# Paged attention of a conditioned residual block: value pages, queries and outputs in 2 KB rows, first key pages requested early

## The reference

```
B, S, HID = 32, 32, 512           # sequences, new tokens of each, features
D, HQ, HK = 128, 32, 8            # head size, query heads, key/value heads
PAGES, PSIZE, NPP = 64, 32, 16    # cache pages, tokens of a page, pages of a sequence
x = x + L0(x); x = x + L1(x); x = x + L2(x)
q, k, v = x @ Wq.T, x @ Wk.T, x @ Wv.T        # 32, 8 and 8 heads of 128
q, k = rope(rmsnorm(q)), rope(rmsnorm(k))
kc = k_cache[block_table]; vc = v_cache[block_table]       # 512 cached tokens of each sequence
scores = q @ concat(kc, k) * SCALE            # 544 keys; cached ones beyond cache_seqlens masked
o = softmax(scores) @ concat(vc, v)
out = x + o @ Wo.T
```

## Time and profile before

| | us |
|---|---|
| median of 3 executions | 1288.35 |
| lowest, highest | 1285.35, 1296.21 |
| the profiled execution | 1295.23 |
| its span (first to last instruction) | 1293.5 |

### The profile page before, as it was taken

The page is one execution under the profiler, slowest core; times in us unless marked ns, Lnnn a source line. Parts: engine busy times, 40 slices in busy tenths (PEclk is TensorE's granted clock), DMA queues, the critical chain, the costliest instruction groups (busy, mean ns, idle before and its releaser), DMA issues. The chain is left out here.

```text
span 1293.5 us, 28328 instructions
## 1 busy us (share of the span) xinstructions
PE 1194.0 (92%) x8010; PEld 1041.7 (81%) x8010; DVE 848.0 (66%) x1756; ACT 678.0 (52%) x1572; POOL 734.5 (57%) x572
## 2 busy tenths in 40 slices
PE   4987999999999699999999999999999994599997
PEld 2733888888888598899989998989899993487786
DVE  3677777777776576777777877777777764322222
ACT  2056444444443476777777777776777764211111
POOL 2030899999999655555555655555655541244442
PEclk9988999999999999999999999999999997799999
DMA  9302344344446699999999999999999946677772
GB/s 298 131 25 91 98 123 133 99 124 131 133 135 196 193 278 272 286 275 288 291 277 284 291 276 283 290 275 286 279 284 294 279 125 224 223 203 216 214 219 86
DMA packets 280080, 275.13 MB, mean 213 GB/s; under 512 B 57285, under 2 KB 242629, under 8 KB 280038
## 3 DMA queue, kind: packets, MB, share of 16 engines
q1 hardware_dynamic: 270278, 250.15, 66.8%
q10 hardware_dynamic: 9504, 24.44, 6.6%
q0 software_dynamic: 256, 0.03, 0.0%
HBM read 228.26 MB, written 46.27 MB: 212 GB/s over the span
## 5 line engine op out<-in xcount | busy, mean ns | idle before, releaser
L1208 ACT ACTIVATE att_prob<-att_neg,att_nmax 128x544 f32<-128x544 f32 x256 | 191.5, 748 | 157.7 <-DVE att_nmax L1028 156.0
L869 POOL TENSOR_TENSOR att_k_lo<-att_kT,att_k_hi 128x544 fp32r<-128x544 f32 x128 | 177.7, 1388 | 143.4 <-ACT att_k_hi L1231 142.7
L869 POOL TENSOR_TENSOR att_k_lo<-all_room_a,att_k_hi 128x544 fp32r<-128x544 f32 x124 | 171.1, 1381 | 128.1 <-ACT att_k_hi L1231 127.5
L1028 DVE CUSTOM_DVE_ANT_1 att_neg<-att_mask,pa_pair 128x576 f32<-128x576 f32 x256 | 192.2, 751 | 73.8 <-PE pa_pair L109 66.1
L1080 DVE COPY att_pT<-pa_pt 128x512 f32<-128x512 f32 x256 | 175.7, 687 | 23.6 <-PE pa_pt L899 23.6
L107 PE MATMUL pa_pair<-prj_wt_hi,early_xT_lo 128*128 128x512 f32 (+1 forms) x512 | 179.9, 351 | 6.4 <-DVE prj_wt_lo L1090 6.4
L108 PE MATMUL pa_pair<-prj_wt_lo,early_xT_hi 128*128 128x512 f32 (+1 forms) x512 | 174.5, 341 | 0.0
L109 PE MATMUL pa_pair<-prj_wt_hi,early_xT_hi 128*128 128x512 f32 (+1 forms) x512 | 172.9, 338 | 0.0
L107 PE MATMUL pa_pair<-att_k_hi,att_q_lo 128*128 128x288 f32 (+1 forms) x512 | 169.1, 330 | 1.1 <-POOL att_k_lo L869 1.1
L1439 POOL TENSOR_TENSOR out_o_n<-out_o_n,all_room_b 128x1024 f32<-128x1024 f32 x32 | 79.1, 2471 | 140.2 <-DMA all_room_b<-inv_scratch 140.2
L899 PE MATMUL pa_pt<-all_ident,att_prob 128*128 128x128 f32 x1024 | 154.0, 273 | 1.5 <-ACT att_prob L1208 1.5
(11 more groups left out here) (143 smaller groups left out, 2623.9 us busy)
## 6 DMA issues: line engine op xcount, KB each, us to landing
all_room_a<-in_k_cache_t SPq DMA_DIRECT2D x256, 128.0 KB, 4.1
att_kT<-in_k_cache_t SPq DMA_DIRECT2D x256, 128.0 KB, 3.5
all_room_b<-in_L_cond_v_cache SPq DMA_DIRECT2D x166, 128.0 KB, 3.5
att_vc<-in_L_cond_v_cache SPq DMA_DIRECT2D x160, 128.0 KB, 3.5
q_scratch<-prj_qst SPq DMA_DIRECT2D x64, 256.0 KB
o_scratch<-att_ost SPq DMA_DIRECT2D x32, 512.0 KB, 5.3
out_o_n<-o_scratch SPq DMA_DIRECT2D x32, 512.0 KB, 3.6
all_room_b<-inv_scratch SPq DMA_DIRECT2D x32, 512.0 KB, 5.7
```

Source lines behind the costliest of these rows:

```text
L869: g.tensor_tensor(k_lo[j % SPLITS][:], kT[j // HK % 2][:, :, j % HK, :], f32(k_hi[j % SPLITS][:]), ALU.subtract).then_inc(k_split, 1)
L1028: v.tensor_tensor_reduce(halves[0], halves[1], ps[j % 2][:, :, 0:KA], 1.0, 3.0e38, ALU.add, ALU.min, nmax[j % 2][:]).then_inc(maxed, 1)
L1208: act.activation(prob[j // GROUP % 2][:, j % GROUP, :], neg[j % 2][:, 0:KEYS], ACT.Exp, bias=nmax[j % 2][:, 0:1], scale=-1.0, accum_out=to ...
```

## The change

Four things are changed.

- **Value pages** lie in SBUF as [half, chunk, four heads x 128] in place of [chunk, eight heads x 128]. A page comes by one DMA as before, but each 4 KB row of it is now two pieces of 2 KB. TensorE's operand is addressed accordingly.
- **Queries** lie in scratch as [batch, d, head, 128] in place of [batch, head, d, 128]; the load of a batch's queries becomes two DMAs, each of four heads (2 KB per partition contiguous on both sides). The stores of the projection still write 512 B runs, now 4 KB apart.
- **Outputs** of a batch are stored by two DMAs of four heads each (2 KB rows), the first between the key pages and the value pages, with waits and semaphores per half.
- **Key pages of batches 0 and 1** (32 DMAs) are no longer requested two by two beside the last two heads' tiles, but all at once before the projection loop.

```
+GROUP = 4
+KQ_LOADS = PG + HK // GROUP
 def load_new_keys(eng, q_d, k_d, b, q, tile, sem):
-    eng.dma_start(q[:], q_d[bass.ds(b, 1)].rearrange("a h d x -> d (a h) x")).then_inc(sem, 16)
+    for g in range(HK // GROUP):
+        h = slice(g * GROUP, (g + 1) * GROUP)
+        eng.dma_start(q[:, h, :], q_d[bass.ds(b, 1), :, h, :].rearrange("a d h x -> (a d) h x")).then_inc(sem, 16)
 def load_value_page(eng, inp, tile, j, page, sem):
-    eng.dma_start(tile[r, j // PPT, :], v_pages[bass.ds(page, 1)].rearrange("a s c -> (a s) c")).then_inc(sem, 16)
+    src = v_pages[bass.ds(page, 1)].rearrange("a s (g x) -> (a s) g x", g=HK // GROUP)
+    eng.dma_start(tile[r, :, j // PPT, :], src).then_inc(sem, 16)
...
-        vc = [vc0, after_w1.sb("vc1", [P, NCH, HK * D])]
+        vc = [vc0, after_w1.sb("vc1", [P, HK // GROUP, NCH, GROUP * D])]
...
-                    sp.dma_start(q_d[tile, bass.ds(c, 1)].rearrange("b a d x -> d (b a) x"),
+                    sp.dma_start(q_d[tile, :, bass.ds(c, 1), :].rearrange("b d a x -> d (b a) x"),
...
                         for i in range(2 * t, 2 * t + 2):
-                            load_key_page(sp, inp, kT[0], i, pages0[i], kq_in[0])
...
-                    elif tail:
-                        for i in range(2 * t, 2 * t + 2):
-                            load_key_page(sp, inp, kT[1], i, pages1[i], kq_in[1])
...
                 pages0 = pages_of(nc, table, 0, 0, NPP, mybir.EngineType.SP)
                 pages1 = pages_of(nc, table, 1, 0, NPP, mybir.EngineType.SP)
+                for i in range(NPP):
+                    load_key_page(sp, inp, kT[0], i, pages0[i], kq_in[0])
+                for i in range(NPP):
+                    load_key_page(sp, inp, kT[1], i, pages1[i], kq_in[1])
                 loop(sp, body)
...
+                def store_out(b, slot, g):
+                    sp.wait_ge(o_staged, b * (HK // GROUP) + g + 3)
+                    cols = slice(g * GROUP * P, (g + 1) * GROUP * P)
+                    sp.dma_start(o_d[bass.ds(b, 1), :, cols].rearrange("a d x -> (a d) x"),
+                                 ost[slot][:, g * GROUP:(g + 1) * GROUP, :].rearrange("p h x -> p (h x)")
+                                 ).then_inc(o_stored[slot * (HK // GROUP) + g], 16)
...
                             load_keys(sp, b + 2, slot, pages)
+                        store_out(b, slot, 0)
+                        if not tail:
                             sp.wait_ge(valued, (b + 1) * HK)
                             load_values(sp, b + 2, slot, pages)
-                        sp.wait_ge(o_staged, (b + 1) * (HK // GROUP) + 2)
-                        sp.dma_start(o_d[bass.ds(b, 1)].rearrange("a d x -> (a d) x"),
-                                     ost[slot][:].rearrange("p h x -> p (h x)")).then_inc(o_stored[slot], 16)
+                        store_out(b, slot, 1)
...
-    q_d = nc.dram_tensor("q_scratch", [B, HK, D, QS], F32).ap()
+    q_d = nc.dram_tensor("q_scratch", [B, D, HK, QS], F32).ap()
```

More of the change, by code:

```diff
@@ L572, in stage_project_attend @@
                          wo, wo_in, q_d, k_d, v_d, o_d, inv_d):
-    GROUP = 4
     UNROLL = 2 * HK
@@ L696, in stage_project_attend @@
         o_staged = m.sem("o_staged")
-        o_stored = [m.sem(f"o_stored{i}") for i in range(2)]
+        o_stored = [m.sem(f"o_stored{i}") for i in range(UNROLL // GROUP)]
         cq, sn_q, ck, sn_k = (tabs[:, i] for i in range(4))
@@ L802, in _ @@
                 pages1 = pages_of(nc, table, 1, 0, NPP, mybir.EngineType.SP)
-                for slot in range(2):
-                    sp.sem_inc(o_stored[slot], 16)
+                for i in range(NPP):
+                    load_key_page(sp, inp, kT[0], i, pages0[i], kq_in[0])
+                for i in range(NPP):
+                    load_key_page(sp, inp, kT[1], i, pages1[i], kq_in[1])
+                for i in range(UNROLL // GROUP):
+                    sp.sem_inc(o_stored[i], 16)
                 loop(sp, body)
@@ L831, in _ @@
                 sp.wait_ge(inv_stored, 32)
+                for i in range(UNROLL // GROUP):
+                    sp.wait_ge(o_stored[i], (B // 2 + 1) * 16)
                 for slot in range(2):
-                    sp.wait_ge(o_stored[slot], (B // 2 + 1) * 16)
                     sp.wait_ge(wo_in[slot], 16)
@@ L913, in values @@
                     s, h = j // HK % 2, j % HK
-                    cols = slice(h * D, (h + 1) * D)
+                    cols = slice(h % GROUP * D, (h % GROUP + 1) * D)
                     o = po[j // GROUP % 2][:, j % GROUP * P:(j % GROUP + 1) * P]
@@ L917, in values @@
                     for c in range(NCH):
-                        pe.matmul(o, vc[s][:, c, cols], pT[j % 2][:, c, :], start=(c == 0 and j % GROUP == 0), stop=False)
+                        pe.matmul(o, vc[s][:, h // GROUP, c, cols], pT[j % 2][:, c, :], start=(c == 0 and j % GROUP == 0), stop=False)
                 def new_values(j, group):
@@ L1044, in split_q_hi @@
                     if g * GROUP % HK == 0:
-                        dve.wait_ge(kq_in[g * GROUP // HK % 2], (it + g * GROUP // UNROLL + 1) * 16 * (PG + 1))
+                        dve.wait_ge(kq_in[g * GROUP // HK % 2], (it + g * GROUP // UNROLL + 1) * 16 * KQ_LOADS)
                     src, hi, lo = q_part(g, it)
@@ L1229, in split_k @@
                     if j % HK == 0:
-                        act.wait_ge(kq_in[j // HK % 2], (it + j // UNROLL + 1) * 16 * (PG + 1))
+                        act.wait_ge(kq_in[j // HK % 2], (it + j // UNROLL + 1) * 16 * KQ_LOADS)
                     act.activation(k_hi[j % SPLITS][:], kT[j // HK % 2][:, :, j % HK, :], ACT.Copy).then_inc(k_hi_done, 1)
@@ L1293, in unit @@
                         act.wait_ge(valued, (group + 1) * GROUP)
-                        if g % 2 == 0:
-                            act.wait_ge(o_stored[j // HK], (it + 1) * 16)
+                        act.wait_ge(o_stored[g], (it + 1) * 16)
                         act.activation(ost[j // HK][:, g % 2 * GROUP:(g % 2 + 1) * GROUP, :],
@@ L1503, in program @@
         kT0 = room_a[:].rearrange("p (j h t) -> p j h t", j=PG, h=HK)
-        vc0 = room_b[:].rearrange("p (c x) -> p c x", c=NCH)
+        vc0 = room_b[:].rearrange("p (g c x) -> p g c x", g=HK // GROUP, c=NCH)
         q0 = m.sb("q0", [P, HK, QS])
```

## The result

| | before | after |
|---|---|---|
| median (us) | 1292.28 | 1328.92 |
| lowest, highest (us) | 1285.35, 1300.12 | 1326.8, 1336.41 |
| ratio to before, 95% interval | | 1.031, 1.0269 to 1.0351 |
| the profiled execution, its span (us) | 1295.23, 1293.5 | 1326.8, 1325.1 |

The changed kernel is 3.1% slower, 36.6 us. The prediction had the direction and 22.5 us of it; the result lies 2 us above the upper end of its range.

A forecast was written before the change was run, and what follows sets the result against it. SyncE's instruction stream was taken as the bound; passes of 20.32 us gave +23.0 us, with -3.0 at the beginning of attention and +2.5 in the projection: +22.5 us, 1310.9 us on the median; 8-in-10 range 1276 to 1327.

The forecast's parts named there:

- What bounds the kernel now: Attention passes: the length of SyncE's instruction stream is the bound, 19.28 us of its own work per pass.
- The second query load: One more DMA in every attention pass, ahead of the key pages: +0.58 us per pass, bounds 0.5 and 0.6.
- the second output store: One more store in every attention pass, register work and wait included: +0.66 us per pass.
- Value pages in two pieces: Ten value page issues per attention pass with one more dimension: +0.015 us each, 0.15 per pass, bounds 0 and 0.3.
- What may come back: Key page issues and table load in SyncE's pass get quicker: 0.35 us per pass taken, of at most 1.9.
- The beginning of attention: With early key pages, SyncE's 4.2 us wait for batch 0's values goes, less 1.24 us of added issues: -3.0 us.
- The beginning of the projection: First tiles: early key pages delay the stores and TensorE stands 3.2 us, bounds 0 and 6; taken as +2.5 us.
- (A): Attention: DMA engines are the bound, not SyncE's issuing; about 1288 us, range 1279 to 1298; chance 0.24.
- (B): Attention: 2 KB rows relieve the DMA engines so much that SyncE's pass shortens; 1267 us, range 1259 to 1279; chance 0.16.
- (C): Attention and projection: nothing comes back and every added cost is at its upper bound; 1329 us; chance 0.10.
- What the profile after would show: Trace signs: passes 20.3 us, no first-pass wait for `valued`, VectorE's waits 78 us, TensorE stall near 155 us, DMA share at most 0.95.

## Why the prediction was right in direction and short by 14 us

**What bounds the kernel now: right where the stream grows.** Three tiny DMAs cost 1.17 us of pass for 1.32 us of SyncE. What the step missed is how near the other limits stand: take work away, and waits for `valued` fill the place. For a change that only adds work this side doesn't matter.

**The second query load, the second output store: right, a little high.** 0.86 - 0.40 = 0.46 us in place of 0.58, and 722.30 - 721.84 = 0.46 in place of 0.66. The estimate of 0.66 had register work in it that isn't repeated.

**Value pages in two pieces: the step that failed.** It took 0.015 us for each page, with an upper bound of 0.03, from the queries' row (0.40 us, three dimensions). Measured: 0.564 - 0.370 = 0.19 us for each, and 5.81 - 4.03 = 1.8 us per pass, twelve times the 0.15 and six times the bound. The queries' DMA fills 128 partitions, and its pieces are apart in HBM alone: in SBUF they lie side by side, the form that the value pages split in HBM later showed to be cheap. So it was no bound for 32 partitions with two pieces 8 KB apart in SBUF, and no row of before shows that form. Two other rows of the kernel before could have warned that the form matters, the projection's stores of queries and of new values:

```profile
L773 SPq DMA_DIRECT2D q_scratch<-prj_qst x64: 387/398/467, 142.6 to 447.8; - x64
...
L778 SPq DMA_DIRECT2D v_scratch<-prj_vst x64: 561/592/1662, 143.8 to 448.8; - x64
```

A store of a single 512 B run per partition costs 592 ns there, more than any load of attention, so an upper bound of 0.03 us on a new form had no row behind it. ScalarE's price (0.258 us more for each of six) wasn't named at all; SyncE's own sums close the pass without it.

**What may come back: too low.** 0.35 us was taken of at most 1.9, with the longer pass named as the reason. Per pass the table load gave back 0.75, the key pages 0.56, the new keys 0.44 - 0.33 = 0.1, in all 1.4 us. The new keys are no relief of the DMA engines: the issue of that unchanged DMA takes 436 to 440 ns at its quickest in all kernels whose queries come in 512 B pieces ahead of it, and 332 ns in all with the new query layout (from 500 us on). Both places named in that step are the right ones, but the slower pace explains only 0.18 us of the key pages (tiny DMAs). The table load is shorter with the split store (alone: 2.24 to 1.39), and the key pages' issues with 2 KB value rows (alone: 6.15 to 5.69).

The two errors are of opposite sign. With the measured terms, 19.28 + 0.46 + 0.46 + 1.78 - 1.4 = 20.58, and 2.9 / 29 = 0.1 of waits: 20.7 us, against 20.79 measured (20.64 from the third pass on) and 20.32 predicted. Without the value pages' error the forecast would have been wrong the other way: the sum had 20.32 - 0.15 = 20.17 us for a cheap form, and the run with one shows 19.19. So the right direction was luck in part: with value pages as cheap as the sum had them, the kernel gets faster, and what made it slower is the term that the sum put at next to nothing.

**The beginning of attention: the mechanism seen, the gain not.** VectorE and SyncE where attention begins, to be read against the earlier trace rows:

```profile
443.39 0.42 DVE L1060 CAST att_q_hi<-att_q 128x512 fp32r<-128x512 f32 x1
...
451.17 0.58 SPq L777 DMA_DIRECT2D q_scratch<-prj_qst  x1
...
458.48 0.89 SPq L541 DMA_DIRECT2D all_q<-q_scratch  x2
...
460.08 9.37 SPq L548 DMA_DIRECT2D all_room_a<-in_k_cache_t  x16
...
470.20 0.56 SPq L742 DMA_DIRECT2D att_vd<-v_scratch  x1
470.86 7.02 SPq L557 DMA_DIRECT2D all_room_b<-in_L_cond_v_cache  x10
```

The stall of 11.50 us ahead of the cast has gone, and so has SyncE's wait for the values of batch 0. But the keys of batch 2 leave at 460.08 in place of 457.25 (the value pages that SyncE issues ahead of them have the dear form too), and the stall comes back one batch later. VectorE's cast for batch 2, then TensorE behind it:

```profile
475.92 0.43 DVE L1060 CAST att_q_hi<-all_q 128x512 fp32r<-128x512 f32 x1 [9.96 <-DMA all_room_a<-in_k_cache_t]
```

```profile
477.98 2.08 PE L931 MATMUL pa_pair<-att_pT,att_vc 128*128 128x128 f32 x8 [6.69 <-DVE att_pT L1093]
```

Before, that cast ran at 471.46 after 0.15 us of waiting. TensorE is then late with the values of batch 1, SyncE waits 2.5 us for them in the second pass, and that pass lasts 24.65 us in place of 19.99. The prediction had named this ("what is late next is that") and priced nothing for it. Up to the third pass's table load its terms give 2.5 - 3.0 + 0.79 = +0.3 us; measured are 503.3 - 497.4 = +5.9. From there on, 28 x (1.17 - 0.79) = 10.6 us are missing. Together the forecast is 16.2 us short by the traces and 14.1 by the medians, a difference within the spread of the last stage.

**The beginning of the projection: right.** SyncE, then TensorE, at the first tiles, beside the earlier trace rows:

```profile
128.73 8.08 SPq L548 DMA_DIRECT2D all_room_a<-in_k_cache_t  x16
136.99 8.05 SPq L548 DMA_DIRECT2D att_kT<-in_k_cache_t  x16
...
146.75 0.41 SPq L777 DMA_DIRECT2D q_scratch<-prj_qst  x1
...
154.89 0.40 SPq L777 DMA_DIRECT2D q_scratch<-prj_qst  x1
...
155.61 1.17 PE L982 MATMUL pa_pair<-all_ident,prj_qn 128*128 128x128 f32 x5 [2.19 <-ACT prj_qst L1281]
```

The stall is there, at the place and by the engine forecast, with 2.19 us for 3.2. The early key pages alone came to +0.2% with an interval around zero, which holds the forecast's -3.0 + 2.5. Their trace speaks against it: the second pass lasts 25.69 us, and the third pass's table load starts at 501.2 us in place of 497.4, so the early pages lose some 4 us. A kernel with the cheap value pages and without the early key pages wasn't run.

**The rivals.** (A) is false for this change: the DMA share fell to 0.89 as the time rose. For a change that shortens the stream TensorE or the DMA engines take over as the limit. (B) is false here, and its mechanism holds as soon as the issue is cheap: the kernel with value pages split in HBM has all other terms of the change and 19.19 us a pass, of which 9.9 / 29 = 0.34 are waits. So 19.28 + 0.46 + 0.46 - 0.13 (value pages 3.90 for 4.03) - 18.85 = 1.2 us came back, against 0.46 + 0.46 - 0.13 = 0.79 us added. (C) has nearly the measured time, 1329, by luck: it had nothing come back, 0.3 us for the value pages and 6 us in the projection.

**What the profile after would show.** Passes of 20.3 us (20.79, or 20.64 from the third on), no wait for `valued` in the first pass (right, but 2.5 us in the second), VectorE's waits 78 us (90.7), a stall near 155 us (right), DMA share at or below 0.95 (0.89). The remark that the table load or the key pages might get much quicker came true, and was outweighed.

**The rules of the Trainium skill.** On the Trainium skill's page DMA: Bandwidth & Descriptors, the section "Issuing engines are not separate DMA queues" calls the issue time usually small beside the DMA itself. The trace differs: a page of 128 KB occupies SyncE for 0.56 us, and at 265 GB/s it is moved in 0.49 us. By the section "Why small descriptors are slow" of the same page of the Trainium skill, as an estimate, the two halves of a 4 KB row cost 134 cycles for 131. The packet records of the traces, 500 to 1000 us, have no such difference: in the mean about 245 ns of a DMA engine for a value row of 4 KB in the kernel before (all 4 KB packets less those of the output stores), and 244 ns for its two halves in the kernel with value pages split in HBM. So the 0.9945 of that kernel doesn't come from cheaper packets.

**What stays open.** Why the value pages' pieces apart in SBUF cost 0.19 to 0.26 us more to issue than pieces apart in HBM: no size, distance or partition count was varied. Being apart in SBUF isn't enough, since the projection's query stores read four pieces 640 B from start to start in each of 128 partitions and are issued in 398 ns. Why 2 KB value rows hold SyncE up less while it issues keys: the runs show that they do, not how. ScalarE's dearer issues were not tested by themselves.

## What to carry to other kernels

Where one engine requests all the data and is never idle, price a change by that engine's time: here each DMA added took its 0.4 to 0.5 us, however few bytes it moved, unless it shortened another wait of that engine, as the split output store did; and each form of DMA that the trace doesn't show is a term of unknown size, times its count in the loop. When requests are moved earlier, ask which transfer is late next, and price that too. Look at the minimum of the issue times, not only the median: a minimum that moves isn't a queue that happens to be full, but the form of that DMA or of the one ahead of it (the new keys, 440 and 332 ns). And before taking work off such an engine, ask what waits next; here 2.24 us fewer in each pass shortened it by 0.51.

## What the runs showed of the hardware

- The issue of a DMA of 32 partitions with two 2 KB pieces each takes 564 ns on SyncE and 580 ns on ScalarE when the pieces lie 8 KB apart in SBUF, and 377 and 323 ns when they lie side by side in SBUF and apart in HBM; one piece of 4 KB takes 370 and 322 ns.
- An unchanged DMA (new keys) is issued in 440 ns right behind one of 1024 pieces of 512 B and in 332 ns behind ones with rows of 2 or 4 KB.
- A store from 128 partitions takes 592 ns to issue with one 512 B run in each (new values), and 398 ns with four such runs, 640 B from start to start in SBUF (queries). The two also differ in how they lie in HBM.
- A 4 KB value row keeps a DMA engine busy for about 245 ns in the mean, and its two halves as packets of 2 KB for 244 ns together.
- A DMA of 512 B costs SyncE as much as one of 512 KB: three of them 1.13 us, one load of queries 0.40 us.
- A load of 16 page numbers into registers takes 0.97 us at its quickest, 2.23 us in the median behind a store of 512 KB, and 1.39 us behind one of 256 KB.
